# Attention block with quads of heads in two row tiles of 64 on TensorE, and one written order per engine

## The reference

```python
def attn(x, w_qkv, b_qkv, w_out, b_out):
    B, L, D = x.shape                      # 32, 512, 256
    H, hd = 16, 16
    bi = jnp.arange(L) // 128              # blocks of 128 tokens
    is_global = bi % 24 == 0               # block 0 alone
    allowed = (bi[:, None] == bi[None, :]) | is_global[:, None] | is_global[None, :]
    mask = jnp.where(allowed, 0.0, -jnp.inf)
    q, k, v = split_heads(x @ w_qkv.T + b_qkv)
    attn = jax.nn.softmax(q * hd ** -0.5 @ k.T + mask, axis=-1)
    return merge_heads(attn @ v) @ w_out.T + b_out
x = x + _layernorm(attn(_layernorm(x), ...))
x = x + _layernorm(relu(_layernorm(x) @ W1 + b1) @ W2 + b2)     # 256 -> 1024 -> 256
```

## Time and profile before

| | before |
|---|---|
| device time, median of 3 runs | 2374.32 us (2372.41 to 2374.86) |
| span of the profiled execution, first to last instruction | 2371.9 us |
| around its span (median run less span) | 2.4 us |
| PE busy / loads of weights (PEld) busy | 97% / 81% |
| DVE busy / ACT busy / POOL busy | 73% / 63% / 33% |
| mean granted TensorE clock | 0.987 of 2.4 GHz |

### The profile page before, as it was taken

The page is one execution under the profiler, slowest core; times in us unless marked ns, Lnnn a source line. Parts: engine busy times, 40 slices in busy tenths (PEclk is TensorE's granted clock), DMA queues, the critical chain, the costliest instruction groups (busy, mean ns, idle before and its releaser), DMA issues.

```text
span 2371.9 us, 59261 instructions
## 1 busy us (share of the span) xinstructions
PE 2296.9 (97%) x18176; PEld 1917.6 (81%) x18176; DVE 1739.7 (73%) x3909; ACT 1487.9 (63%) x3077; POOL 781.8 (33%) x1159
## 2 busy tenths in 40 slices
PE   5899999999999999999999999999999999999997
PEld 3678888888888888888888888888888888888876
DVE  5777777777777777777777777777777777777742
ACT  3456666666666666666666666666666666666654
POOL 0023332333332333332333332333332333332344
PEclk8989999999999999999999999999999999999998
DMA  6444444344444444444344444444444444444410
GB/s 141 95 85 80 87 87 93 78 88 78 86 86 93 78 88 78 86 85 92 79 88 78 86 85 92 79 88 79 86 85 92 79 88 79 86 85 84 82 33 18
DMA packets 158659, 197.93 MB, mean 83 GB/s; under 512 B 37392, under 2 KB 88336, under 8 KB 158600
## 3 DMA queue, kind: packets, MB, share of 16 engines
q1 hardware_dynamic: 107400, 146.83, 34.4%
q10 hardware_dynamic: 51200, 50.34, 6.7%
HBM read 37.25 MB, written 16.78 MB: 23 GB/s over the span
## 4 chain that ended last, share of the span: by engine, by line
PE 88%; DVE 5%; DMA 3%; issue 2%; ACT 1%; POOL 1%; SPq 0%; DVEq 0%; POOLq 0%; ACTq 0%
PE p_lin L425 29%; PE p_lin L490 15%; PE p_max L359 8%; PE p_o L408 7%; PE p_sc L383 7%; PE p_max L354 6%; PE p_o L405 5%; PE p_sc L378 5%; PE p_lin L417 3%; DMA stack<-max_row 2%; PE p_lin L453 2%; DVE neg_max L646 2%; PE p_lin L438 1%; DVE max_row L677 1%; POOL h_lo L789 1%
## 5 line engine op out<-in xcount | busy, mean ns | idle before, releaser
L533 ACT ACTIVATE probs<-p_sc 128x512 f32<-128x512 f32 x1280 | 725.3, 603 | 590.4 <-PE p_sc L378 317.2
L646 DVE TENSOR_REDUCE neg_max<-p_max 128x2 f32<-128x512 f32 (+1 forms) x1280 | 856.0, 679 | 192.3 <-PE p_max L359 112.7
L789 POOL TENSOR_TENSOR h_lo<-h_f,h_hi 128x256 fp32r<-128x256 f32 x512 | 364.9, 732 | 512.1 <-ACT h_hi L571 505.9
L359 PE MATMUL p_max<-stack 72*128 72x256 f32 x1536 | 341.6, 304 | 19.5 <-DVE neg_max L646 19.2
L571 ACT ACTIVATE h_f<-p_lin,b_s 128x256 f32<-128x256 f32 x512 | 243.4, 475 | 120.7 <-PE p_lin L425 120.3
L359 PEld LDWEIGHTS p_max<-stack 72*128 72x128 f32 x1536 | 244.0, 191 | 89.6 <-issue 52.2
L383 PE MATMUL p_sc<-stack 80*128 80x256 f32 x1536 | 310.2, 284 | 0.0
L425 PE MATMUL p_lin<-x_hi,w_hi 128*128 128x256 f32 (+1 forms) x1280 | 297.3, 314 | 3.7 <-ACT h_hi L571 2.0
L490 PE MATMUL p_lin<-w_hi,h_hi 128*128 128x256 f32 x1024 | 292.6, 286 | 7.2 <-POOL h_lo L789 6.0
L383 PEld LDWEIGHTS p_sc<-stack 80*128 80x128 f32 x1536 | 273.8, 192 | 28.9 <-ACT probs L533 0.7
L490 PE MATMUL p_lin<-w_lo,h_hi 128*128 128x256 f32 x1024 | 291.2, 284 | 0.0
(11 more groups left out here) (81 smaller groups left out, 3767.2 us busy)
## 6 DMA issues: line engine op xcount, KB each, us to landing
stack<-qk SPq DMA_DIRECT2D x2048, 64.0 KB, 2.3
xa<-x ACTq DMA_DIRECT2D x32, 512.0 KB, 3.9
xr<-x ACTq DMA_DIRECT2D x32, 512.0 KB, 3.5
out<-yf ACTq DMA_DIRECT2D x64, 256.0 KB, 2.5
stack<-max_row SPq DMA_DIRECT2D x256, 32.0 KB
probs<-w SPq DMA_DIRECT2D x2, 512.0 KB, 4.7
probs<-w_qkv_t SPq DMA_DIRECT2D x2, 384.0 KB, 5.0
x_old<-w SPq DMA_DIRECT2D x1, 512.0 KB, 6.9
```

Source lines behind the costliest of these rows:

```text
L359: last = nc.tensor.matmul(dst[:, j * 2 * P:(j + 1) * 2 * P].rearrange("p (a n) -> p a n", a=2), q_stack[0:MAXROW, buf, j, kb * P:(kb + 1) ...
L533: nc.scalar.activation(probs[:, CH * (p % 2) + c, :], p_sc[k % 2][:, :], ACT.Exp, scale=SCALE).then_inc(exp_done, 1)
L646: nc.vector.tensor_reduce(dst, src, axis=AX.X, op=ALU.max, negate=True).then_inc(red_done, 1)
L789: last = nc.gpsimd.tensor_tensor(h_parts[1][:, m, :], h_f[:, n % 2, u, :], h_parts[0][:, m, :].bitcast(F32), ALU.subtract)
```

## The change

Heads now go in quads, made of two pairs. The stack has no buffers but one place for each of the 8 pairs; the two heads of a pair stand in partitions 0 to 48 and 64 to 112 (`ROW` = 64): three hi/lo terms of 16 rows (the product of the two low parts is left out) and one row of the maximum. A matmul for head j uses only rows 64j and up, and writes bank j of a pair of banks. A pass therefore has two matmuls of 512 or four of 256, fills two banks, and there are 20 passes of each kind in a batch, not 40. `p_max` and `p_sc` are one bank pair each, so that a pass waits for the reader of the pass before it. VectorE's maximum and ScalarE's exp read 1,024 columns each. The maxima are transposed by four transposes a quad, copied (`copy_max`) and moved by two DMAs. The rows of ones and the mask rows of the stack are gone; `load_stack` has 6 DMAs a pair, not 8. The values product of a quad stands in one piece (`pv`). `xh` is gone (ln2 is applied in place). Loads of x and stores are issued by SyncE, not by ScalarE. The one table of slots becomes one written order for each engine (`ORDER`), of which the first lines are shown.

```diff
-SCHEDULE = {
-    (0, 0): [("mt", 7, -1), ("x2t", 1, -2), ("ln1_mean", 0, 1)],
...
+ORDER = {
+    "PE": [
+        ("v", 1, 0), ("o_t", 3, -1), ("x1", 0, 1), ("x1", 1, 1), ("scores", 1, 0), ("scores_max", 8, 0),
...
-        stack = sb("stack", [P, BUFS, 2, 2, L], F32R)
+        stack = sb("stack", [P, 2, PAIRS, L], F32R)
...
-        p_max = [ps(f"p_max{j}", [P, L]) for j in range(2)]
-        p_sc = [ps(f"p_sc{j}", [P, L]) for j in range(2)]
+        p_max = ps("p_max", [P, 2, L])
+        p_sc = ps("p_sc", [P, 2, L])
...
-                    for n in range(4):
-                        a, c = n % 2, 2 + n // 2
-                        sp.dma_start(stack[n * HD:(n + 1) * HD, buf, :, j, :].bitcast(F32),
+                    for m in range(3):
+                        a, c = m % 2, 2 + m // 2
+                        at = ROW * j + m * HD
+                        sp.dma_start(stack[at:at + HD, :, n, :].bitcast(F32),
...
+            def scores(dst, quad, c, stationary, moving, rows):
+                for m, (pair, kb, col) in enumerate(step_parts(c)):
+                    at = 2 * quad + pair
+                    for j in range(2):
+                        r = slice(ROW * j, ROW * j + rows)
+                        if kb == 0:
+                            last = nc.tensor.matmul(dst[:, j, :], stack[r, stationary, at, 0:P],
+                                                    stack[r, moving, at, :], start=True, stop=True)
+                        else:
+                            last = nc.tensor.matmul(
+                                dst[:, j, col:col + HALF].rearrange("p (a n) -> p a n", a=2),
+                                stack[r, stationary, at, kb * P:(kb + 1) * P],
+                                two(stack[r, moving, at, :], kb), start=True, stop=True)
...
-                wait(pe, red_done, i, PC, k - 1)
+                    wait(pe, red_done, b, QC, n)
+                    scores(p_max, quad, c, 0, 1, STACK).then_inc(max_mm, 1)
...
-                wait(pe, exp_done, b, PC, k - 1)
+                    wait(pe, exp_done, b, QC, n)
+                    scores(p_sc, quad, c, 1, 0, K_ALL).then_inc(sc_mm, 1)
...
+                if what == "pv":
+                    wait(pe, ev["v"], b, 2, 2)
+                    wait(pe, ot_done, b, QUADS, n)
+                    wait(pe, exp_done, b, QC, CH * (n + 1))
+                    for kb in range(KB):
+                        for h in range(4):
...
-                nc.scalar.activation(probs[:, CH * (p % 2) + c, :], p_sc[k % 2][:, :], ACT.Exp,
-                                     scale=SCALE).then_inc(exp_done, 1)
+                    nc.scalar.activation(probs[:, prob_slot(quad, c), :, :], p_sc[:, :, :], ACT.Exp,
+                                         scale=SCALE).then_inc(exp_done, 1)
```

More of the change, by code:

```diff
@@ L216, in there, with first @@
             return not isinstance(b, int) or 0 <= b < NB
-        def above(b, k):
-            return not isinstance(b, int) or b > 0 or k > 0
+        def first(b, n):
+            return isinstance(b, int) and b == 0 and n == 0
         def wait(eng, s, b, per, k):
@@ L235, in bank_of, with bank @@
             return at % len(UNITS) % LIN
+        def bank(what, which):
+            return p_lin[bank_of(place(what, which))]
         def unit_before(what, which, i):
@@ L365, in scores @@
-            def scores(i, s, t):
-                b, p, c = second(i, s, t)
-                if not there(b):
-                    return
-                buf, k = p % BUFS, CH * p + c
-                if c == 0:
-                    wait(pe, row_in, b, 128, 16 * (p + 1))
-                wait(pe, exp_done, b, PC, k - 1)
-                dst = p_sc[k % 2]
-                if c < 2:
-                    last = nc.tensor.matmul(dst[:, :], k_stack[0:K_ALL, buf, c, 0:P],
-                                            q_stack[0:K_ALL, buf, c, :], start=True, stop=True)
-                else:
-                    kb = c - 1
-                    for j in range(2):
-                        last = nc.tensor.matmul(
-                            dst[:, j * 2 * P:(j + 1) * 2 * P].rearrange("p (a n) -> p a n", a=2),
-                            k_stack[0:K_ALL, buf, j, kb * P:(kb + 1) * P],
-                            two(q_stack[0:K_ALL, buf, j, :], kb), start=True, stop=True)
-                last.then_inc(sc_mm, 1)
@@ L455, in job @@
                 elif what == "qk":
[L456 removed]
+                    if first(b, n):
                         pe.wait_ge(lo_split, 1)
[L458 removed]
+                    wait(pe, ev["x1"], b, 2, 2)
                     col = O_QKV + (n % 2) * D + (n // 2) * P
@@ L463, in job @@
                 elif what == "v":
+                    if first(b, n):
+                        pe.wait_ge(lo_split, 1)
+                    wait(pe, ev["x1"], b, 2, 2)
                     for u in range(2):
@@ L494, in job @@
                 last.then_inc(mm[what], 1)
-            def step(i):
-                for s in range(SLOTS):
-                    for t in range(TURNS):
-                        if there(i):
-                            scores_for_max(i, s, t)
-                        scores(i, s, t)
-                        for what, n, off in SCHEDULE.get((s, t), []):
-                            if what in LINEAR and there(i + off):
-                                job(i, what, n, i + off)
-                        for kb in PV_TURNS.get(t, ()) if s % 2 == 1 else ():
-                            probs_x_values(i, s, kb)
@@ L558, in job @@
                         for p in range(4 * (n // 2), 4 * (n // 2) + 4):
-                            for j in range(2):
-                                wait(act, stack_in[p][j], b, 64, 0)
-                    nc.scalar.activation(qk[:, n // 2, 2 * (n % 2), :], src[:, :], ACT.Identity,
+                            wait(act, stack_in[p], b, 96, 0)
+                    nc.scalar.activation(qk[:, n // 2, 2 * (n % 2), :], bank("qk", n)[:, :], ACT.Identity,
                                          bias=bqk_s[:, n:n + 1]).then_inc(hi_done["qk"], 1)
-                elif what == "f1":
+                    if n == 1 and isinstance(b, int) and b == 0:
+                        split_rest()
+                elif what == "relu":
                     half = n // 4
@@ L597, in job, with split_first @@
                     last.then_inc(norm_done[kind], 1)
[L599 to L611 removed]
+            steps(act, ORDER["ACT"], job)
         @block.vector
         def _(dve):
[L616 removed]
+            def split_first():
                 dve.wait_ge(hi_split, 1)
@@ L749, in step @@
-            def step(i):
-                for s in range(SLOTS):
-                    for t in range(TURNS):
-                        for what, n, off in SCHEDULE.get((s, t), []):
-                            if what.endswith("_mean") and there(i + off):
-                                wait(dve, bn_done[what[:3]], i + off, 2, n + 1)
-                        if there(i):
-                            maxima(i, s, t)
-                        for what, n, off in SCHEDULE.get((s, t), []):
-                            if there(i + off):
-                                job(what, n, i + off)
@@ L765, in _, with statistics_done @@
+            def statistics_done(what, following):
+                for next_what, n, b in () if what.endswith("_mean") else following:
+                    if not next_what.endswith("_mean"):
+                        break
+                    wait(dve, bn_done[next_what[:3]], b, 2, n + 1)
+            steps(dve, ORDER["DVE"], job, statistics_done)
         @block.gpsimd
```

667 lines of the change are left out of this document (323 added, 344 removed), and 26 rows, old and new, of the table SCHEDULE.

## The result

| | before | after |
|---|---|---|
| device time, median of 4 runs each, same chip | 2374.59 us (2372.41 to 2375.7) | **2297.57 us** (2294.88 to 2298.4) |
| ratio, 95% interval | | 0.9677 [0.9663, 0.9691] |
| span of the profiled execution | 2371.9 us | 2293.1 us |
| one batch | 71.12 us | 69.12 us in the hardware loop, 68.21 us in the batches written out ahead of it and behind it |
| mean granted TensorE clock | 0.987 | 0.986 |

What follows compares the result with a forecast made beforehand. TensorE's instruction stream was taken as the bound: 71.1 - 9.6 - 1.2 + 0.3 - 0.8 + 6.5 = 66.3 us a batch, with 2.0 of waits 68.3; 32 x 68.3 + 96.1 and 2.4 gave 2284 us, range 2110 to 2480.

Steps and rivals of the forecast that it cites:

- Passes at once: TensorE's passes: both heads of a pair stream at once in separate row halves, 40 passes replacing 80, -9.6 us a batch.
- Values in one piece: TensorE's values products: 4 excursions into their array form and back a batch, not 8, -1.2 us.
- Transposes of the maxima: TensorE: 16 transposes of the maxima a batch instead of 8, at 0.075 us each, +0.3 us.
- Bare loads after transposes: TensorE: most places with an unhidden weight load after transposes become form changes, -0.8 us a batch.
- Borders: TensorE: 35 new array form changes a batch between half-row passes and full-row units, about 0.195 us each, +6.5 us.
- Waits: TensorE's waits with single bank pairs and no slack from maxima pass 7 to 14: +2.0 us a batch, bounds 0 and 7.
- 20.4 and 20.3 us: Predicted work of VectorE and of TensorE from maxima pass 7 to 14, neither having slack.
- A: Rival: row tiles on TensorE change form for free; 2150 us, chance 0.20.
- B: Rival: weight loads of a pair's two heads queue on one load path; slower, 2479 us, chance 0.13.
- C: Rival: single bank pairs cost more, 4 to 7 us of waits a batch; 2348 to 2444 us, chance 0.09.
- D: Rival: row tiles run one after the other; 2361 us with free form changes, 2543 with paid ones, chance 0.06.

Runs made afterwards that it cites:

- Run 1: Changed kernel with both heads of a pair on rows 0 to 48, so their matmuls cannot run at once, form borders kept: 2564.78 us.
- run 11: Changed kernel, hardware loop kept, with the values product again in two pieces and one pass between them: 2342.6 us.
- run 2: Changed kernel with every pass on rows 0 to 71, heads one after the other, 35 of 43 form borders a batch gone: 2381.0 us.
- Run 4: Changed kernel with VectorE taking the maxima of head 0 alone, 512 columns and not 1024: 2261.48 us.
- run 9: Changed kernel, loop written out, exp 4 moved ahead of qk_hi 2 on ScalarE and ln2_mean 0 ahead of qk_lo 2 on VectorE: 2293.47 us.
- run 12: Changed kernel, loop written out, VectorE's ln2_mean 1 moved ahead of the maximum of pass 13: 2261.29 us.
- run 5: Kernel before the change with 64 unused bytes a partition ahead of o_n, so o2, x2 and h start 64 bytes later: 2359.57 us.
- run 6: Changed kernel with 64 unused bytes a partition ahead of o_n, putting o2, x2 and h at multiples of 128 bytes: 2318.39 us.
- run 3: Changed kernel with passes on rows 0 to 71 and head 1's matmuls left out after the first batch: 2223.82 us.
- run 8: Changed kernel with the x2 transposes moved behind scores pass 7 and o_t 0, with neighbours on ScalarE and VectorE moved to fit: 2303.46 us.
- run 10: As run 9, with x1 high and low also beginning 64 bytes beyond a multiple of 128: 2314.64 us.
- run 7: Changed kernel with the hardware loop replaced by all 32 batches written out: 2275.89 us.

## Why the prediction was right, point by point

The sum was 68.3 us a batch. Measured are 69.12 in 19 batches (the loop's) and 68.21 in the other 13, on average 68.75, so the ends are 2293.1 - 32 x 68.75 = 93.1 us against 96.1. The median lies 13.6 us over the forecast: 32 x 0.45 = 14.4 of batches, -3.0 of ends, and the rest is the distance from the span to the median.

1. **Passes at once, -9.6:** right. Run 1 gives -9.0, and the trace shows 1024 columns in one streaming of 0.23 us.
2. **Values in one piece, -1.2:** right (run 11: about 0.3 us per excursion).
3. **Transposes of the maxima, +0.3:** too small. They start every 0.108 us with 4 columns as with 128, so 16 cost 1.7 and the term is +0.8. I had taken a value between the bounds where the upper one, the nearest row, was right. The reading behind it was wrong: I took the 0.11 us between transposes for the time of the load, but with loads of 4 columns the distance is the same, so it isn't the load that sets it. That a load of 128 columns does take about as long is seen elsewhere: four loads in two rounds take 0.30 us, one round 0.19.
4. **Bare loads after transposes, -0.8:** not tested by itself.
5. **Borders, +6.5:** right in kind, a tenth too high; runs 1 and 2 give 5.8, 0.165 for each and not 0.195.
6. **Waits, +2.0:** too small by 0.6 in the loop, where the list of waits gives 2.6 us; about 1.9 written out. The place was right (passes 7 to 14, second LayerNorm), and so were the *sums* of work that I had compared: 20.4 and 20.3 us, measured 20.53 and 20.65. (The 0.3 in TensorE's sum has no name there.) What sums can't give is the size of each wait, and there the reason was only half. Run 4 leaves half of the largest wait though VectorE has time to spare, run 9 shows that ScalarE's order makes the second, run 12 that 0.5 us of the x2 wait were one round trip to GpSimd behind a long instruction.
7. **Missing altogether:** the loop's own cost, by the code its register waits, which an engine that becomes critical no longer hides (+0.9 us a batch in the loop, of which 0.7 are already in the x2 wait of point 6), and the closer spacing of 256-wide products (15 to 21 us less, runs 5 and 6, 0.5 to 0.7 a batch).

With what was measured the sum is 71.1 - 9.0 - 1.2 + 0.8 - 0.8 + 5.8 - 0.6 + 2.6 = 68.7 us, against 69.12 in the loop; 0.4 of it has no term. The mechanism was right, but that the forecast came within 14 us is partly luck. It was too low by 0.6 in the streams at once, 0.5 in the transposes, 0.6 in the waits (the loop's share among them) and these 0.4. Against that stand 0.7 too much for the borders and 0.6 for a spacing that no one had aimed at.

**The rivals.** A is out: the borders are there. Its price was wrong too (run 3: 2224, not 2150). B is out: the loads of the halves don't queue. C was right that waits are more than I charged, not that they pass 4 us. D is out: run 1 is what it would have looked like, 2565 us (some 2540 without the clock's falls) against 2543 in its working.

## What to carry to other kernels

Row tiles pay by the length of a run in one form: here 40 streamings of 0.24 us were saved and 35 borders at 0.165 us paid, and two thirds of the gain went. Count the borders in the order of the engine before you count the columns.

Once two engines are near each other, ask for each step between them which *short* instruction with a round trip (to GpSimd, to ScalarE) stands behind a long one. Moving that one instruction brought 15 us in the kernel written out; leaving out half of the long ones had brought 36 in the looped one, and moving a wait from one place to another cost 6 and 18 us (runs 8 and 9). And try the loop written out as soon as TensorE no longer covers what it costs the other engines: 22 us here.

## What the hardware showed that I had not expected

- Behind the wait before the transposes of x2, TensorE's clock falls in some batches from 2.4 to 1.2 GHz for a few us (6.6 in the one shown): in 5 batches with a wait of 1.5 us (run 9), in 11 with the same wait (run 10), in 7 with a wait of only 1.0 (run 1), in 3 with 1.4 (run 3), and in none with the same 1.4 in the kernel after. The length of the wait alone doesn't decide it.
- 256-wide fp32r products start every 113 to 120 ns, depending on where tensors lie, which no one chose for that: 15 us to 21 us by one pad of 64 bytes (runs 5 and 6). The rule behind it stays open.
- Transposes with 4 stationary columns start every 0.108 us, no sooner than those with 128.
- In the hardware loop some of VectorE's instructions start 0.1 to 0.2 us later behind the same neighbour than written out (run 7).
